# Two stacked transformer layers: probabilities and values as pairs of 16-bit parts, masks on TensorE, projection one round later, roots on GpSimd

## What is computed

```python
def _layer(x, wqkv, qs, ksc, wo, lg, lb, w1, b1, w2, b2):
    h = shift_token(x)                    # half of the features from the token before
    q, k, v = jnp.split(h @ wqkv, 3, axis=-1)     # 8 heads of 64
    q = l2norm(q) * qs; k = l2norm(k) * ksc
    q, k = rotary_xpos(q, k)
    o = local_attention(q, k, v)          # window 128: a block and the one before it, softmax
    x = x + o @ wo
    h = shift_token(x)
    h = (h - mu) / jnp.sqrt(var + 1e-05) * lg + lb
    a, g = jnp.split(h @ w1 + b1, 2, axis=-1)     # 682 hidden features each
    return x + (a * gelu(g)) @ w2 + b2
...
x = x + _L0_attn_ref(xn, ...) + _L0_ffn_ref(xn, ...)
```

## Time and profile before

| | |
|---|---|
| median of 3 runs | 3972.04 us (3971.88 to 3972.2) |
| the profiled execution | 3974.68 us, span 3972.9 us |
| busy: TensorE, VectorE, ScalarE, GpSimd | 3510.6, 2638.4, 2148.6, 1522.5 us |
| a round of the layers' loops | 81.84 us |
| mean granted TensorE clock | 0.96 |

### The profile page before, as it was taken

How to read it: one execution, slowest core, us unless ns; L and a number is a source line. 1 busy time by engine, 2 the same in 40 slices (tenths; PEclk the granted TensorE clock), 3 DMA queues, 4 the chain that set the end, 5 groups by cost and what they waited for, 6 DMA issues and landing times.

```text
span 3972.9 us, 72434 instructions
## 1 busy us (share of the span) xinstructions
PE 3510.6 (88%) x26976; PEld 2099.6 (53%) x26976; DVE 2638.4 (66%) x4180; ACT 2148.6 (54%) x2585; POOL 1522.5 (38%) x1584
## 2 busy tenths in 40 slices
...
GB/s 56 48 60 54 58 55 57 56 56 57 45 82 6 14 21 19 18 34 19 21 18 18 34 19 42 20 50 19 27 24 24 34 35 25 24 27 31 37 19 35
DMA packets 149003, 139.02 MB, mean 35 GB/s; under 512 B 11132, under 2 KB 147376, under 8 KB 148912
## 3 DMA queue, kind: packets, MB, share of 16 engines
...
...
## 4 chain that ended last, share of the span: by engine, by line
issue 29%; POOL 21%; PE 15%; DVE 4%; ACT 2%; POOLq 0%; DMA 0%; SPq 0%; DVEq 0%; ACTq 0%
POOL f_u L1478 7%; POOL f_u L1483 5%; PE f_p L1104 3%; PE f_p L1123 3%; POOL f_hT L1494 3%; POOL f_Pl L1502 2%; PE f_p L1145 2%; PE f_p L1023 2%; POOL f_xb L1511 2%; PE f_p L1086 2%; POOL f_Pl L1504 1%; POOL f_qst L1488 1%; PE f_p L1090 1%; POOL f_mark_l L1499 1%; DVE f_negm L1360 1%
## 5 line engine op out<-in xcount | busy, mean ns | idle before, releaser
L654 DVE TENSOR_REDUCE m_negm<-m_p 128x2 f16<-128x1024 f32 x512 | 608.3, 1221 | 170.4 <-PE m_p L473 168.5
L576 ACT ACTIVATE m_Pr<-m_p 128x1024 f32<-128x1024 f32 x512 | 500.6, 1020 | 163.9 <-PE m_p L492 159.4
L1478 POOL TENSOR_TENSOR f_u<-f_u,f_bt 128x1024 f32<-128x1024 f32 x128 | 301.9, 2358 | 561.2 <-DVE f_bt L1332 561.2
L1104 PE MATMUL f_p<-f_vl,f_Pl 128*128 128x65 f32 x3584 | 426.1, 279 | 30.7 <-POOL f_Pl L1504 30.7
L1104 PEld LDWEIGHTS f_p<-f_vl,f_Pl 128*128 128x128 f32 x3584 | 416.0, 195 | 41.0 <-POOL f_Pl L1504 31.4
L1229 ACT ACTIVATE f_Pl<-f_p 128x896 f32<-128x896 f32 x256 | 220.5, 914 | 328.8 <-PE f_p L1090 221.6
L1494 POOL TENSOR_TENSOR f_hT<-f_gates,f_hT 128x512 f16<-128x512 f32 x192 | 223.8, 1166 | 396.5 <-ACT f_gates L1252 395.1
L501 PE MATMUL m_o<-m_Pr,m_vm 128*32 128x512 f32 x2048 | 341.6, 645 | 13.0 <-ACT m_Pr L576 13.0
L1023 PE MATMUL f_p<-f_wq_h,f_xT_h 128*128 128x512 f16 x768 | 295.8, 385 | 62.4 <-DVE f_mark_x L1318 45.1
L1244 ACT ACTIVATE f_gates<-f_p,f_bias 128x512 f32<-128x512 f32 x192 | 131.4, 684 | 344.8 <-PE f_p L1145 344.7
L1360 DVE TENSOR_REDUCE f_negm<-f_p 128x4 bf16<-128x1024 f32 x256 | 295.7, 1222 | 15.0 <-PE f_p L1056 15.0
...
## 6 DMA issues: line engine op xcount, KB each, us to landing
...
m_QT<-m_hi SPq DMA_DIRECT2D x128, 64.0 KB
m_KT<-m_hi SPq DMA_DIRECT2D x128, 64.0 KB
...
```

Source lines behind the costliest of these rows:

```text
L576: act.activation(Pr[kt % 2][:, 2 * u:2 * u + 2, :].rearrange("p h t -> p (h t)"), psum[w.slot("M2", g, kt, u)][:, :], ACT.Exp).then_inc(*w ...
L654: dve.tensor_reduce(negm[:, t, pr // 2, :, pr % 2], psum[w.slot("M1", h, u)][:, :].rearrange("p (a k) -> p a k", a=2), AX.X, ALU.max, nega ...
L1104: mm = pe.matmul(psum[w.slot("PV", hp)][:, e * T + t * (DH + 1):e * T + (t + 1) * (DH + 1)], Pl[h % 4][:, at * W:(at + 1) * W], vl[:, j, h ...
L1478: pool.tensor_tensor(u[t][:], u[t][:], bt[:], ALU.add).then_inc(*bt_used.up(I))
```

## The change

- `Pl` becomes two f32 tiles; ScalarE writes the exponential there (now waiting for the low part of the head two before), copies it to f16 as the high part (`PH`, new step), and VectorE subtracts to get the low part (`PL`, new step). `vl` becomes f16: high part, ones column, low part, the latter by VectorE (`V`). PV issues three f16 products for one in f32.
- The selects on GpSimd go; L2 gets eight matmuls with the mask matrix.
- OT and WO move from stream C to a new stream D that works on sequence i-2, one round later, in the same round as that sequence's LX, LN and XH. The section late has D too.
- RN and the LayerNorm's root (new step LR, with the application LA apart from LN) move to GpSimd, as a power and one Newton step; SH moves there as well.
- The sixth hidden tile's values and gates are made by one set of products, 42 gates in rows 0 to 41 and 42 values in rows 64 to 105.
- The gated product has three buffers, not two; wo is staged in the probabilities' tile by its own load (WS) and split at other places. All five order lists are rewritten.

```diff
-        "POOL": """A.QK,0 A.QK,1 A.QK,2 A.QK,3 F.H1,0 F.H1,1 F.H1,2 A.NM,0 F.H1,3 F.H1,4 F.H1,5 A.SQ,0 C.L2,0 C.L2,1 A.NM,1 C.L2,2 C.L2,3
...
+        "POOL": """A.QK,0 A.QK,1 A.QK,2 F.H1,0 A.QK,3 A.RN A.NM,0 F.H1,1 A.SQ,0 A.SH,0 F.H1,2 F.H1,3 F.H1,4 F.H1,5 A.NM,1 N.LR A.SQ,1
...
-        Pall = sb("Pl", [P, 4, NK], F32)
-        Pl = [Pall[:, r, :] for r in range(4)]
+        Pl = [sb(f"Pl{r}", [P, NK], F32) for r in range(2)]
+        Pall = sb("Ph", [P, 4, 2, NK], F16)
+        Pp = [Pall[:, r] for r in range(4)]
...
-        gates, hT = sb("gates", [P, 4, T], F32), sb("hT", [P, 2, NF, T], F16)
-        G, hp_ = [[gates[:, 2 * n + r, :] for r in range(2)] for n in range(2)]
+        gates, hT = sb("gates", [P, 5, T], F32), sb("hT", [P, 2, NF, T], F16)
+        G, hp_ = [gates[:, r, :] for r in range(2)], [gates[:, 2 + r, :] for r in range(3)]
...
-        st_o = u[NT - 1].rearrange("p (f n) -> p f n", f=NP_)
+        st_o = Pall[:].rearrange("p r e k -> p (r e k)").bitcast(F32)[:, 0:NP_ * D].rearrange("p (f n) -> p f n", f=NP_)
...
+                for e in range(2):
+                    for j in range(NT):
+                        pe.matmul(dst(e, j), identb[:], masks[:].rearrange("p a k -> p (a k)")[:, 0:min(2 * W, T - j * W)],
+                                  start=False, stop=False, skip_group_check=True)
...
-                pe.wait_ge(*masked.at(I, 2 * (2 * hp + 2)))
+                pe.wait_ge(*p_lo_ready.at(I, 2 * hp + 2))
                 pe.wait_ge(*w.is_free("PV", hp))
                 for e in range(2):
                     h = 2 * hp + e
                     for t in range(NT):
                         for j in range(max(t - 1, 0), t + 1):
                             at = 2 * j + t - j
-                            mm = pe.matmul(psum[w.slot("PV", hp)][:, e * T + t * (DH + 1):e * T + (t + 1) * (DH + 1)],
-                                           Pl[h % 4][:, at * W:(at + 1) * W], vl[:, j, h, :], start=(t == 0), stop=(j == t),
-                                           skip_group_check=True)
+                            dst = psum[w.slot("PV", hp)][:, e * T + t * (DH + 1):e * T + (t + 1) * (DH + 1)]
+                            p_hi, p_lo = [Pp[h % 4][:, part, at * W:(at + 1) * W] for part in range(2)]
+                            pe.matmul(dst, p_hi, vl[:, j, h, 0:DH + 1], start=(t == 0), stop=False, skip_group_check=True)
+                            pe.matmul(dst[:, 0:DH], p_hi, vl[:, j, h, DH + 1:], start=False, stop=False, skip_group_check=True)
+                            mm = pe.matmul(dst, p_lo, vl[:, j, h, 0:DH + 1], start=False, stop=(j == t), skip_group_check=True)
                 mm.then_inc(*w.fills("PV", hp))
 
             def ot(I, half):
-                w.wait(w.is_drained("PV", 2 * half + 1), w.is_free("OT", half))
+                pe.wait_ge(*on_ready.at(I, half + 1))
+                pe.wait_ge(*w.is_free("OT", half))
...
+                if f == NF - 1:
+                    for c in range(NC):
+                        for k, (a_, b_) in enumerate(((wt_h, xhT_h), (wt_l, xhT_h), (wt_h, xhT_l))):
+                            mm = pe.matmul(psum[w.slot("W1", f)][0:HALF + TAIL, 0:T], a_[:, c, :], b_[:, c, :],
+                                           start=(c == 0 and k == 0), stop=(c == NC - 1 and k == 2))
+                    mm.then_inc(*w.fills("W1", f))
...
             def l2(I, hp):
+                for h in (2 * hp, 2 * hp + 1):
+                    act.wait_ge(*w.is_full("L2", h))
+                    if h >= 2:
+                        act.wait_ge(*p_lo_ready.at(I, h - 1))
+                    act.activation(Pl[h % 2][:], psum[w.slot("L2", h)][:, 0:NK], ACT.Exp, scale=1 / KBOOST)\
+                        .then_inc(*w.frees("L2", h))
+
+            def p_hi(I, hp):
                 if hp >= 2:
                     act.wait_ge(*w.is_full("PV", hp - 2))
                 for h in (2 * hp, 2 * hp + 1):
-                    act.wait_ge(*w.is_full("L2", h))
-                    act.activation(Pl[h % 4][:], psum[w.slot("L2", h)][:, 0:NK], ACT.Exp, scale=1 / KBOOST)\
-                        .then_inc(*w.frees("L2", h))
+                    act.wait_ge(*w.is_drained("L2", h))
+                    act.activation(Pp[h % 4][:, 0, :], Pl[h % 2][:], ACT.Copy).then_inc(*p_hi_ready.up(I))
...
-            def rn_(I):
-                def link(ins):
-                    ins.then_inc(*rn_link.up(I))
-                    dve.wait_ge(*rn_link.now(I))
-
-                def flat(m):
-                    return m[:].rearrange("p t h -> p (t h)")
-                dve.wait_ge(*ss_ready.at(I, NT))
-                dve.wait_ge(*u_ready.before(I, 1))
-                link(dve.tensor_scalar(flat(ss), flat(ss), (NORM_MIN * WSCALE) ** 2, None, ALU.max))
-                rsqrt(dve, link, flat(ss), flat(rn), flat(rt))
-                dve.memset(mark_v[:], 0.0).then_inc(*rn_ready.up(I))
-
-            def sh(I, t):
-                dve.wait_ge(*hi_ready.at(I, t + 1))
-                dve.tensor_tensor(klt[t][:].rearrange("p (h d) -> p h d", h=H), u[t][:, INNER:].rearrange("p (h d) -> p h d", h=H),
-                                  khh[t][:, :, 0:DH], ALU.subtract).then_inc(*stack_ready.up(I))
+                if t == NT - 1:
+                    dve.wait_ge(*ss_ready.at(I, NT))
+                    dve.tensor_scalar(ss[:].rearrange("p t h -> p (t h)"), ss[:].rearrange("p t h -> p (t h)"), (NORM_MIN * WSCALE) ** 2,
+                                      None, ALU.max).then_inc(*ss_bounded.up(I))
+
+            def v_(I, t):
+                dve.wait_ge(*v_hi_ready.at(I, t + 1))
+                dve.scalar_tensor_tensor(vl[:, t, :, DH + 1:], psum[w.slot("V", t)][:, 0:INNER].rearrange("p (h d) -> p h d", h=H),
+                                         1 / WSCALE, vl[:, t, :, 0:DH], ALU.mult, ALU.subtract).then_inc(*w.frees("V", t))
+
+            def p_lo(I, hp):
+                for h in (2 * hp, 2 * hp + 1):
+                    dve.wait_ge(*p_hi_ready.at(I, h + 1))
+                    dve.tensor_tensor(Pp[h % 4][:, 1, :], Pl[h % 2][:], Pp[h % 4][:, 0, :], ALU.subtract).then_inc(*p_lo_ready.up(I))
...
+            def roots(link, v, y, t):
+
+                def factor(n):
+                    return factors[:, n:n + 1].to_broadcast([P, v.shape[1]])
+                link(pool.tensor_tensor(y, v, factor(1), ALU.pow))
+                link(pool.tensor_tensor(t, y, y, ALU.mult))
+                link(pool.tensor_tensor(t, t, v, ALU.mult))
+                link(pool.tensor_tensor(t, t, factor(2), ALU.mult))
+                link(pool.tensor_tensor(t, factor(3), t, ALU.subtract))
+                return pool.tensor_tensor(y, y, t, ALU.mult)
+
+            def rn_(I):
+                def link(ins):
+                    ins.then_inc(*rn_link.up(I))
+                    pool.wait_ge(*rn_link.now(I))
+
+                def flat(m):
+                    return m[:].rearrange("p t h -> p (t h)")
+                pool.wait_ge(*ss_bounded.at(I, 1))
+                roots(link, flat(ss), flat(rn), flat(rt)).then_inc(*rn_ready.up(I))
+
+            def lr(I):
+                def link(ins):
+                    ins.then_inc(*rstd_link.up(I))
+                    pool.wait_ge(*rstd_link.now(I))
+                pool.wait_ge(*mv_ready.at(I, 1))
+                link(pool.tensor_tensor(var[:], mv[:, :, 1], factors[:, 0:1].to_broadcast([P, NT]), ALU.add))
+                roots(link, var[:], rstd[:], tmp[:]).then_inc(*rstd_ready.up(I))
+
+            def sh(I, t):
+                pool.wait_ge(*hi_ready.at(I, t + 1))
+                pool.tensor_tensor(klt[t][:].rearrange("p (h d) -> p h d", h=H), u[t][:, INNER:].rearrange("p (h d) -> p h d", h=H),
+                                   khh[t][:, :, 0:DH], ALU.subtract).then_inc(*stack_ready.up(I))
...
-            def l2(I, hp):
-                for h in (2 * hp, 2 * hp + 1):
-                    pool.wait_ge(*w.is_drained("L2", h))
-                    pool.tensor_tensor(mark_l[:, h:h + 1], mark_p[:], mark_p[:], ALU.add)
-                    own = Pl[h % 4][:].rearrange("p (j k) -> p j k", k=W)[:, 0:2 * NT - 1:2, :]
-                    nxt = Pl[h % 4][:].rearrange("p (j k) -> p j k", k=W)[:, 1:2 * NT - 1:2, :]
-                    pool.affine_select(out=own, in_=own, compare_op=ALU.is_ge, fill=0.0, base=0,
-                                       pattern=[[0, NT], [1, W]], channel_multiplier=-1).then_inc(*masked.up(I))
-                    pool.affine_select(out=nxt, in_=nxt, compare_op=ALU.is_ge, fill=0.0, base=0,
-                                       pattern=[[0, NT - 1], [-1, W]], channel_multiplier=1).then_inc(*masked.up(I))
...
+            def ws(I):
+                if I.b > 0:
+                    hold(on_ready.at(all_of_layer(I.b), 0))
+                load(I, wo_loaded, st_o, wo[I.b].rearrange("(c p) n -> p c n", p=P))
```

More of the change, by code:

```diff
@@ L811, in layers_phase @@
+        "SP": """A.XT F.W2,0 F.W2,1 N.LX F.W2,2 C.XR N.XH""",
     }
```

129 lines of the change are left out of this document (70 added, 59 removed).

## The result

| | before | changed |
|---|---|---|
| median of 4 runs | 3972.12 us | 4220.39 us (4214.94 to 4231.8) |
| ratio to before | | 1.0625 (95%: 1.061 to 1.0641) |
| span of the profiled execution | 3972.9 us | 4213.2 us |
| a round, mean of twelve: first layer, second layer | 81.84, 81.87 us | 89.07, 92.07 us |
| mean granted TensorE clock | 0.96 | 0.92 |

The changed kernel is 6.2% slower; 3864 us was forecast. It is rival C, the power that grows with its columns, at a somewhat lower price (10.5 us, not 13.3) and with two costs on top that no term of the prediction had.

The account below looks back on a forecast made before the run. TensorE's stream was taken to bound the round: 72.4 us plus about 5.6 of waits, 78.0. 26 rounds save 99 us, filling and draining 12, the end costs 3: minus 108 from 3972.04 gives 3864 us, range 3812 to 3985.

Parts of the forecast that it names:

- rival C: GpSimd's 64-column power grows with its columns; at 13.3 us it adds 12.0 a round, 4195 us, slower; chance 0.19.
- 42 narrow products: TensorE's f16 products of probabilities and values: 42 start within 1.4 us; 168 a round cost 5.5 us, 7.3 less.
- Eight masks: Mask matmuls added on TensorE for each pair of heads: 0.77 us, plus 3.1 us a round for four pairs.
- The stream without waits: Sum of TensorE's matmuls in a round: from 77.9 to 72.4 us, ends 71.9 and 76.3.
- the walk: The new order followed through a round with row prices: TensorE waits about 5.6 us, against 3.9 before; round 78.0 us.
- (a): TensorE's wait for the split transposed input: 1.5 us with handoff, 0.6 remaining after 0.9 of output transposes.
- (b): TensorE's wait in C.ST,2 for its second PSUM tile, used by D.OT,1 and freed by VectorE: about 1.7 us.
- the power of 64 columns: GpSimd's power for the root of the norms, before NM,0: taken as 1.3 us, from 1.018 us at 4 columns.
- the two bounds: For GpSimd's power of 64 columns: 1.1 us if the excess is fixed, 13.3 us if all by column.
- the free part: In GpSimd's chain before HI,0, a power of 1.0 us is free; each us more costs one every round.
- D: Rival with a middle price for GpSimd's power, 2.5 to 4.5 us: 3900 to 3965 us; chance 0.09.
- a last section: After the loop's tail, the last projection now precedes the shift, LayerNorm and last gates: 3 us more.

Follow-up runs that it names:

- e6_split: Changed kernel with the norms' root cut into two 32-column powers on GpSimd and N.LS at the end of GpSimd's round; 3883.43 us, 0.9767 of before.
- e4_pow16: Changed kernel with GpSimd's power of the norms on 16 of 64 columns, the others filled with copies; 3945.3 us in one run.
- e9_three: e6_split with the root cut at 48 and 16 columns and NM,2 moved before N.LR; 3846.2 us, 0.9676 of before.

## Why the prediction was wrong

**Point by point.** What it said of TensorE held. 42 narrow products, from one round:

```profile
2007.28 0.20 PE L1113 MATMUL f_p<-f_vl,f_Ph 128*128 128x65 f16 x1
...
2008.67 0.39 PE L1085 MATMUL f_p<-f_mT,f_sel 32*128 32x256 bf16 x8
```

That is 1.39 us, 33 ns each; 1.4 and 33 were forecast. Eight masks take 0.78 us (1999.97 to 2000.75; 0.77). The stream without waits is 72.4 us (72.4; the 78.17 us of e6_split less 5.8 of waits). The waits that the walk found are there: (a) 0.48 and (b) 1.60 us idle, against 0.6 and 1.7:

```profile
1942.40 0.39 PE L1026 MATMUL f_p<-f_wq_h,f_xT_h 128*128 128x512 f16 x1 [0.48 <-DVE f_mark_x L1345]
...
1954.83 0.34 PE L1043 MATMUL f_p<-f_ident,f_klt 128*128 128x128 f16 x3 [1.60 <-DVE f_oT_l L1406]
```

**The step that failed** is the value for the power of 64 columns: 1.3 us, from "the row at 4 columns is nearest". A single row can't tell a fixed excess from one by the column, and the two bounds were 12 us apart on the chain in front of HI,0. It took 10.53, and four widths show that it grows by the column (0.159 us). The walk itself was right: by it NM,0 ends at 44.0 + 10.5 = 54.5 us, 9.5 after the 45.0 at which HI,0 has to start, and TensorE waited 8.6 (the free part was 1.9, not 1.0). That this was a rival with 0.19, and left outside the range, is the error of weighing that went with it. (The range is said to end with D, which by its own line ends at 3965; it was given as 3985. The measured time lies beyond both.)

**Two terms were missing.** Rival C at 10.53 us would give a round of 78.0 + 9.5 = 87.5 and some 4130 us; it was 4220. The first is the port between VectorE and GpSimd: LS and NM,2 were looked at for their work and their order, and not for what VectorE does beside them. The prediction even had the output store late ("issued only at 65") and didn't ask what waits for it, which is LS. Moving LS away gives 101 us. The second is TensorE's clock: the wait of 8.44 us costs itself and, in every round, matmuls at the 1.2 GHz level behind it. The 60 first ones take 6.97 to 8.24 us, where e4_pow16 has 5.52: 1.45 us more in a usual round of the first layer, 2.05 in one of the second. The two work together: in the second layer LS and NM,2 catch two scalings and not one, the clock is at its lower level behind that wait in eleven rounds of twelve (behind the 2.66 us of the first layer in one of eleven), the mean clock is 0.91 and not 0.95, and the round is 3.0 us longer.

**The counter-test.** With the power in gaps and LS away (e6_split) the usual round is 78.17 us, 78.0 forecast, with waits of 5.8 us, 5.6 forecast; the time is 3883, 3864 forecast, the rest being rounds of 79.6 now and then and a last section that is 5.5 us longer than before (3 forecast). That the waits agree is in part luck: the last of them is 2.17 us because NM,2 meets the last low parts, which no term had; without that (e9_three) it is 0.69, and the round 77.63. So the stream's sum was right; what was wrong was one instruction's price, and what was missing the port and the clock.

**Where the 240 us of the span are.** 24 round spacings give 86.7 + 122.5 = 209 us, the sections before, between and behind the loops 31, of which 20 are behind the last loop round (5.5 in e6_split); what makes up the 31 is open.
